# A dense phase on one Trainium2 core: fp32 products against three fp32r products of parts, and the order of its two layers

## What is computed

```python
o = o.reshape(b, n, n, D) @ W_out
h = layer_norm(x + o, ln_agg_g, ln_agg_b)
m = jax.nn.relu(h @ W1 + b1) @ W2 + b2
return layer_norm(m + h, ln2_g, ln2_b)
```

## Time and profile before

| | |
|---|---|
| median of 3 runs | 4186.32 us |
| the profiled execution | 4186.14 us |
| its span | 4184.3 us |
| TensorE busy (PE) | 3655.8 us, 87% of the span |
| VectorE busy (DVE) | 2901.9 us, 69% |
| ScalarE busy (ACT) | 2311.9 us, 55% |
| GpSimd busy (POOL) | 1372.4 us, 33% |

### The profile page before, as it was taken

How to read it: one execution, slowest core, us unless ns; L and a number is a source line. 1 busy time by engine, 2 the same in 40 slices (tenths; PEclk the granted TensorE clock), 3 DMA queues, 4 the chain that set the end, 5 groups by cost and what they waited for, 6 DMA issues and landing times. The chain is left out here.

```text
span 4184.3 us, 80451 instructions
## 1 busy us (share of the span) xinstructions
PE 3655.8 (87%) x29631; PEld 2959.3 (71%) x29631; DVE 2901.9 (69%) x4154; ACT 2311.9 (55%) x5686; POOL 1372.4 (33%) x730
## 2 busy tenths in 40 slices
PE   8873888688869997899999978999999777788887
PEld 5542666466648884788888856888888744688886
DVE  2657999699966772577777743777777644577787
ACT  3423777577754553466656643666666411477776
POOL 0355999799964441100000001000000000122254
PEclk9986999899989998999999999999999999999999
DMA  4365111411123333000000011000000133545565
GB/s 127 93 156 139 42 44 41 110 44 40 41 61 96 101 96 95 26 16 16 16 18 24 11 55 61 16 16 16 16 16 11 33 125 133 164 137 137 143 203 173
DMA packets 211175, 304.39 MB, mean 73 GB/s; under 512 B 18656, under 2 KB 156768, under 8 KB 210272
## 3 DMA queue, kind: packets, MB, share of 16 engines
q1 hardware_dynamic: 201696, 292.56, 23.5%
q10 hardware_dynamic: 9216, 8.39, 0.6%
HBM read 200.22 MB, written 100.66 MB: 72 GB/s over the span
## 5 line engine op out<-in xcount | busy, mean ns | idle before, releaser
L611 DVE TENSOR_TENSOR mp_Z<-mp_psL,mx_rv 128x2816 f32<-128x2816 f32 (+1 forms) x256 | 786.7, 3149 | 46.1 <-DMA mx_rv<-rv 25.2
L631 POOL TENSOR_TENSOR mp_Z<-mp_lvs,mx_rv 128x1280 f32<-128x1280 f32 (+1 forms) x256 | 797.0, 3730 | 64.5 <-ACT mp_lvs L554 39.8
L561 ACT ACTIVATE mp_cut<-mp_psO,mx_mask 128x128 f32<-128x128 f32 x2048 | 550.1, 403 | 157.1 <-PE mp_psO L504 157.1
L504 PE MATMUL mp_psO<-mp_Z,mp_pair 128*16 128x256 f32 x8192 | 504.7, 387 | 106.8 <-POOL mp_Z L631 93.6
L1164 PE MATMUL sv_psO<-at_v_hi,sv_p_hi 128*128 128x258 f32 x2048 | 583.3, 285 | 13.2 <-DVE sv_p_lo L1252 10.1
L1164 PE MATMUL sv_psO<-at_v_lo,sv_p_hi 128*128 128x258 f32 x2048 | 578.2, 282 | 0.0
L1164 PE MATMUL sv_psO<-at_v_hi,sv_p_lo 128*128 128x258 f32 x2048 | 577.9, 282 | 0.0
L1183 ACT COPY sv_S<-sv_psS 128x512 f32<-128x512 f32 x512 | 300.5, 587 | 395.1 <-PE sv_psS L1138 289.6
L504 PEld LDWEIGHTS mp_psO<-mp_Z,mp_pair 128*16 128x16 f32 x8192 | 339.6, 124 | 247.3 <-DVE mp_Z L611 135.3
L1227 DVE TENSOR_TENSOR sv_run<-sv_run,sv_S 128x512 f32<-128x512 f32 x448 | 314.5, 702 | 249.5 <-ACT sv_S L1183 249.0
L1252 DVE TENSOR_TENSOR sv_p_lo<-sv_S,sv_p_hi 128x512 fp32r<-128x512 f32 x512 | 353.8, 691 | 107.9 <-ACT sv_p_hi L1192 106.9
(11 more groups left out here) (199 smaller groups left out, 6888.5 us busy)
## 6 DMA issues: line engine op xcount, KB each, us to landing
re_xg<-xg SPq DMA_DIRECT2D x192, 384.0 KB, 3.3
xg<-ga_xg SPq DMA_DIRECT2D x32, 768.0 KB, 3.7
mp_pair<-att SPq DMA_DIRECT2D x128, 128.0 KB, 2.6
fr_xr<-in_x SPq DMA_DIRECT2D x16, 512.0 KB, 4.8
fr_xl<-in_x SPq DMA_DIRECT2D x32, 256.0 KB, 4.2
rv<-fr_rvs SPq DMA_DIRECT2D x16, 512.0 KB, 2.9
att<-mx_rv SPq DMA_DIRECT2D x16, 512.0 KB, 6.8
att<-fr_E SPq DMA_DIRECT2D x16, 512.0 KB, 6.4
```

Of the source, the lines that this page charges most:

```text
L504: mm = pe.matmul(psO[32 * j:32 * j + 2 * H, c % 2, q, :], pair[:, s, :, :, c * YC + y], Z[:, c, y, :], start=True, stop=True, tile_positio ...
L561: ins = nc.scalar.activation(cut[:, s, c, :, h * DK:(h + 1) * DK], psO[:, c % 2, :, h * DK:(h + 1) * DK], ACT.Copy, scale=mask[:, h:h + 1])
L611: nc.vector.tensor_tensor(Z[:, c, 0:m], psL[:, s, 0:D].unsqueeze(1).broadcast_to([P, m, D]), rv[:, c * YC:c * YC + m, :], ALU.mult).then_i ...
L631: nc.gpsimd.tensor_tensor(Z[:, c, m:YC], lvs[:, s, :].unsqueeze(1).broadcast_to([P, YC - m, D]), rv[:, c * YC + m:(c + 1) * YC, :], ALU.mu ...
```

## The change

Output projection and inner layer are made of three fp32r products each. The weights are split once, `wo_hi`, `wo_lo`, `wa_hi`, `wa_lo`. Per tile, ScalarE makes the high parts `oT_hi` and `hT_hi`, and VectorE the low parts `oT_lo` and `hT_lo`. `hT` no longer has the first norm's shift; its product with W1 is made once (8 products of one column) and added to b1, as `b1s`. The transposes of the input move to one round earlier, behind the output projection (`turn_o`), and the loads with them. The outer layer moves ahead of the inner one. `xoff` becomes two instructions of one column. An `xl`, `xT`, relu or root is as before.

```diff
@@ -655,16 +655,19 @@
...
+        wo_hi, wo_lo = (ph.sb(n, [P, KT, D], F32R) for n in ("wo_hi", "wo_lo"))
+        wa_hi, wa_lo = (ph.sb(n, [P, KT, F1], F32R) for n in ("wa_hi", "wa_lo"))
...
         g1c, b1nc = (ph.sb(n, [P, KT]) for n in ("g1c", "b1nc"))
         b1c = ph.sb("b1c", [P, MT])
+        b1s = ph.sb("b1s", [P, MT])
...
-        oT = ph.sb("oT", [P, 2, KT, W])
+        oT_hi, oT_lo = (ph.sb(n, [P, 2, KT, W], F32R) for n in ("oT_hi", "oT_lo"))
...
-        hT = ph.sb("hT", [P, 2, KT, W])
+        hT_hi, hT_lo = (ph.sb(n, [P, 2, KT, W], F32R) for n in ("hT_hi", "hT_lo"))
...
@@ -728,13 +732,19 @@
...
                 ox = o_d.rearrange("b n (y x) d -> (b n) x y d", x=2)
+
+                def load(i):
+                    reach(sp, o_turned, i - 1)
+                    reach(sp, added1, i - 1)
+                    for c in range(2):
+                        sp.dma_start(oin[c * N:(c + 1) * N, i % 2], ox[i * U:(i + 1) * U, c].rearrange("u y d -> y u d")).then_inc(in_[i % 2], 16)
+                    sp.dma_start(xres[:, i % 2], tile_rows(x.rearrange("b x y d -> (b x y) d"), i)).then_inc(in_[i % 2], 16)
+
+                load(0)
+                load(1)
                 for i in range(LAST + 1):
-                    if i < NT:
-                        reach(sp, o_turned, i - 1)
-                        reach(sp, added1, i - 1)
-                        for c in range(2):
-                            sp.dma_start(oin[c * N:(c + 1) * N, i % 2], ox[i * U:(i + 1) * U, c].rearrange("u y d -> y u d")).then_inc(in_[i % 2], 16)
-                        sp.dma_start(xres[:, i % 2], tile_rows(x.rearrange("b x y d -> (b x y) d"), i)).then_inc(in_[i % 2], 16)
+                    if i + 2 < NT:
+                        load(i + 2)
                     n = i - 4
                     if 0 <= n < NT:
                         sp.wait_ge(t_made, n + 1)
@@ -755,18 +765,30 @@
...
+                def parts(k):
+
+                    return ((0, 0, k), (0, 1, k), (1, 0, k))
+
...
+                oTs, wos, hTs, was = (oT_hi, oT_lo), (wo_hi, wo_lo), (hT_hi, hT_lo), (wa_hi, wa_lo)
                 pe.wait_ge(w_in, 16 * len(loads))
+                for f in range(MT):
+                    for k in range(KT):
+                        mm = pe.matmul(ps_m[:, f, 0:1], wa[:, k, f * P:(f + 1) * P], b1nc[:, k:k + 1], start=(k == 0), stop=(k == KT - 1))
+                mm.then_inc(b1_turned, 1)
+
+                def turn_o(i):
+                    pe.wait_ge(in_[i % 2], (i // 2 + 1) * 48)
+                    reach(pe, oT_kept, i)
+                    turn(ps_o, oin[:, i % 2], o_turned)
+
+                turn_o(0)
                 for i in range(LAST + 1):
-                    if i < NT:
-                        pe.wait_ge(in_[i % 2], (i // 2 + 1) * 48)
-                        reach(pe, oT_kept, i)
-                        turn(ps_o, oin[:, i % 2], o_turned)
                     n = i - 1
                     if 0 <= n < NT:
                         pe.wait_ge(ln[H_LN]["normed"], n + 1)
@@ -780,22 +802,34 @@
                     if i < NT:
                         pe.wait_ge(oT_kept, i + 1)
                         reach(pe, added1, i)
-                        by_token(ps_1, oT[:, i % 2], wo, KT, made1)
-                    n = i - 1
-                    if 0 <= n < NT:
-                        pe.wait_ge(hT_kept, n + 1)
-                        for f in range(MT):
-                            if f % 2 == 0:
-                                reach(pe, mT_made, (n - 1) * 2 + f // 2 + 1)
-                            for k in range(KT):
-                                mm = pe.matmul(ps_m[:, f, :], wa[:, k, f * P:(f + 1) * P], hT[:, n % 2, k, :], start=(k == 0), stop=(k == KT - 1))
-                            if f % 2 == 1:
-                                mm.then_inc(made2, 1)
+                        reach(pe, w_cut, 1)
+                        for u in range(U):
+                            terms = [t for k in range(KT) for t in parts(k)]
+                            for e, (a, c, k) in enumerate(terms):
+                                mm = pe.matmul(ps_1[:, u * D:(u + 1) * D], oTs[a][:, i % 2, k, u * P:(u + 1) * P], wos[c][:, k, :],
+                                               start=(e == 0), stop=(e == len(terms) - 1))
+                        mm.then_inc(made1, 1)
+                    if i + 1 < NT:
+                        turn_o(i + 1)
                     n = i - 2
                     if 0 <= n < NT:
                         pe.wait_ge(mT_made, n * 2 + 2)
                         reach(pe, added3, n)
                         by_token(ps_3, mT[:, n % 2], wb, MT, made3)
+                    n = i - 1
+                    if 0 <= n < NT:
+                        pe.wait_ge(hT_kept, n + 1)
+                        pe.wait_ge(w_cut, 2)
+                        pe.wait_ge(b1_made, 1)
+                        for f in range(MT):
+                            if f % 2 == 0:
+                                reach(pe, mT_made, (n - 1) * 2 + f // 2 + 1)
+                            terms = [t for k in range(KT) for t in parts(k)]
+                            for e, (a, c, k) in enumerate(terms):
+                                mm = pe.matmul(ps_m[:, f, :], was[c][:, k, f * P:(f + 1) * P], hTs[a][:, n % 2, k, :],
+                                               start=(e == 0), stop=(e == len(terms) - 1))
+                            if f % 2 == 1:
+                                mm.then_inc(made2, 1)
 
             @block.scalar
             def _(act):
@@ -808,17 +842,24 @@
 
...
+                nc.scalar.copy(wo_hi[:, :, :], wo[:, :, :]).then_inc(w_hi_cut, 1)
+                nc.scalar.copy(wa_hi[:, :, :], wa[:, :, :]).then_inc(w_hi_cut, 1)
+
+                def keep_oT_hi(i):
+                    act.wait_ge(o_turned, i + 1)
+                    reach(act, made1, i - 1)
+                    keep(oT_hi[:, i % 2], ps_o, oT_hi_kept)
+
+                keep_oT_hi(0)
                 for i in range(LAST + 1):
-                    if i < NT:
-                        act.wait_ge(o_turned, i + 1)
-                        keep(oT[:, i % 2], ps_o, oT_kept)
                     n = i - 1
                     if 0 <= n < NT:
                         act.wait_ge(h_turned, n + 1)
                         for k in range(KT):
-                            ins = nc.scalar.activation(hT[:, n % 2, k, :], ps_h[:, k * W:(k + 1) * W], ACT.Identity,
-                                                       bias=b1nc[:, k:k + 1], scale=g1c[:, k:k + 1])
-                        ins.then_inc(hT_kept, 1)
+                            ins = nc.scalar.activation(hT_hi[:, n % 2, k, :], ps_h[:, k * W:(k + 1) * W], ACT.Copy, scale=g1c[:, k:k + 1])
+                        ins.then_inc(hT_hi_kept, 1)
+                    if i + 1 < NT:
+                        keep_oT_hi(i + 1)
                     n = i - 3
                     if 0 <= n < NT:
                         root(T_LN, n)
@@ -834,10 +875,11 @@
                         root(X_LN, n)
                     n = i - 1
                     if 0 <= n < NT:
+                        act.wait_ge(b1_made, 1)
                         for f in range(MT):
                             if f % 2 == 0:
                                 act.wait_ge(made2, n * 2 + f // 2 + 1)
-                            ins = nc.scalar.activation(mT[:, n % 2, f, :], ps_m[:, f, :], ACT.Relu, bias=b1c[:, f:f + 1])
+                            ins = nc.scalar.activation(mT[:, n % 2, f, :], ps_m[:, f, :], ACT.Relu, bias=b1s[:, f:f + 1])
                             if f % 2 == 1:
                                 ins.then_inc(mT_made, 1)
                     n = i - 4
@@ -871,12 +913,35 @@
                 nc.vector.memset(eps[:, :], LN_EPS).then_inc(eps_set, 1)
                 dve.wait_ge(w_in, 16 * len(loads))
                 nc.vector.tensor_tensor(hbr[:, :], b1nr[:, :], b2r[:, :], ALU.add).then_inc(hbr_made, 1)
+                for j, (lo, full, hi) in enumerate(((wo_lo, wo, wo_hi), (wa_lo, wa, wa_hi))):
+                    dve.wait_ge(w_hi_cut, j + 1)
+                    nc.vector.tensor_tensor(lo[:, :, :], full[:, :, :], hi[:, :, :], ALU.subtract).then_inc(w_cut, 1)
+                dve.wait_ge(b1_turned, 1)
+                nc.vector.tensor_tensor(b1s[:, :], ps_m[:, :, 0], b1c[:, :], ALU.add).then_inc(b1_made, 1)
+
+                def keep_oT_lo(n):
+                    dve.wait_ge(oT_hi_kept, n + 1)
+                    nc.vector.tensor_tensor(oT_lo[:, n % 2], ps_o[:, :].rearrange("p (k t) -> p k t", k=KT), oT_hi[:, n % 2], ALU.subtract).then_inc(oT_kept, 1)
+
+                def keep_hT_lo(n):
+                    dve.wait_ge(hT_hi_kept, n + 1)
+                    for k in range(KT):
+                        ins = nc.vector.scalar_tensor_tensor(out=hT_lo[:, n % 2, k, :], in0=ps_h[:, k * W:(k + 1) * W], scalar=g1c[:, k:k + 1],
```

(19 more changed lines are left out.)

## The result

The changed kernel takes **4200.89 us** (median of 6 runs, 4198.33 to 4204.64) against 4185.11 us of the kernel before (6 runs, 4182.99 to 4189.31): a ratio of 1.0037, 95% interval 1.0024 to 1.0050. It is slower by 16 us. The forecast was 4208, in a range of 4198 to 4221. By time alone the effect is small, 0.4%, and the profile has to show where it comes from.

What follows compares the result with a forecast made beforehand. TensorE bounds the dense phase at 10.01 us a round; the move closes a loop of 10.95, so 28 rounds x 0.94 = +26.3, less 3 to 4 in the drain, together +22: 4208 us, range 4198 to 4221.

Steps and rivals of the forecast that it cites:

- The bound and the products: Dense phase: TensorE is the bound at 10.01 us a round; 12 products fall from 5.24 to 4.32 us as fp32r.
- TensorE's own work: TensorE's work in a dense round after the change: 9.08 us, or 9.24 with changes from fp32 to fp32r.
- The loop: Inner layer's end, relus 3 and 4, xl, ps_x transposes, TensorE's next round; TensorE idles about 1.6 us a round at ps_x.
- the loop's length: Time of one turn through relus, xl and TensorE: 10.87 us, 11.0 with type changes, taken as 10.95 a round.
- the two changes of type: Switches from fp32 to fp32r products on TensorE, 0.08 us lost at each of two a round.
- The transposes after a wait: Four ps_x transposes on TensorE after waiting for xl: 0.44 + 0.16 = 0.60 us.
- The second loop: From ps_x transposes through output projection, oT_hi cast, second norm's root, VectorE's norms, relus and xl: 10.75 us, 10.83 with one type change.
- The count and the drain: 28 rounds x 0.94 = +26.3 us; three last tiles drain through the norms with xoff freed, -3 to -4.
- the rival of overlaps: Overlapping steps and hand-overs shorten the loop to 10.0 to 10.3 us a round: 4182 to 4195 us; chance 7%.
- VectorE's new work: Added per round on VectorE: oT_lo 0.72 us, hT_lo pair 0.9; xoff becomes 0.3 for both instructions.
- TensorE stays the bound: Rival: ScalarE finishes relus 3, 4 and xl within the 0.44 us of ps_h transposes: 4157 us; chance 4%.
- xoff held all the same: Rival: GpSimd's multiply still holds xoff to 1.3 us, xl starts 0.9 later each round: 4233 us; chance 9%.

Runs made afterwards that it cites:

- b1: Changed kernel with ps_x transposes between outer and inner layer on TensorE, and xl one round later behind hT_hi on ScalarE; 4157.06 us, ratio 0.9935.
- e5: Changed kernel with xl made between relus 1, 2 and relus 3, 4 on ScalarE; 4184.46 us, ratio 0.9997.
- e1: Changed kernel with the ps_x transposes moved behind the next input's transposes, ahead of the outer layer; 4177.15 us, ratio 0.9983.
- e3: Kernel before, fp32 throughout, with only the outer layer moved ahead of the inner one; 4221.93 us, ratio 1.0095.
- e2: Changed kernel with the inner layer put back ahead of the outer layer on TensorE; 4189.14 us, ratio 1.0011.
- e6: e2 with the second norm's root put ahead of the cast to oT_hi on ScalarE; 4176.46 us, ratio 0.9978.
- e4: Kernel before with only xoff made as two instructions of one column; 4184.2 us, one run.
- e7: Changed kernel with xoff again made by one scalar_tensor_tensor, as in the kernel before; 4208.2 us, one run.

## Why the prediction was right, and where it was off

- **The bound and the products** held. TensorE's own work was put at 9.08 to 9.24; b1 shows 9.05. The fp32r products start 0.119 us apart (1405.48 to 1408.09, 22 steps), against my 0.12. The Trainium skill ("TensorE: Matmul & The Clock Gate", Back-to-back issue gap) gives an isolated warm gap of N/2.4 + 2.5 ns, 109 ns for 256 columns; the trace does not agree, by 10 ns a product.
- **The loop** held in every link: the two last relus, xl, ps_x, released by xl 31 times. The wait is 51.1 us in total; I had some 1.5 x 28 = 42. A steady round shows 1.47, and the rest is longer waits in the drain (5.75 us the longest). Three runs show that it was this chain: in e5 the round falls by 0.62 when two relus move, in e1 the wait for xl is gone from the steady rounds when the transposes move, and in e3 the order alone makes it.
- **The term that was mis-sized most is the loop's length**, "10.87, and 11.0 with the two changes of type ... I take 10.95". It is 10.74. The transposes after a wait cost 0.41 to the next product, not 0.44 + 0.16: 0.19 less. The added 0.16 was taken from the length of the last record, while the start of what follows is what counts. A change of type costs about nothing net: the output projection is 0.08 longer, but outer and inner layer together are 6.31 where I had 6.33 without a change. 10.87 - 0.19 + 0.08 - 0.02 = 10.74. I chose 0.21 too much, 5.5 us over 26 rounds.
- **The second loop** was shorter too, 10.26 in e2 against 10.75, mostly VectorE: 4.00 against 4.35. In the changed kernel it has slack, seen as the 0.37 that ScalarE waits for relus 3 and 4. That it is real is shown by e2, and by e6, which opens it.
- **The count and the drain.** 26 rounds are at the full length, not 28 (1.9 us). The drain gained 1.0 us up to the last xl, and lost 0.4 behind it (9.10 us to the end of the phase against 8.71), against my 3 to 4. e4 shows the size of the reason that I gave: freeing xoff alone brings the drain 1.0, not 1.0 for each of three tiles. In the changed kernel the drain differs in more than xoff: its last outer layer also took 1.7 us longer at the lower clock. So the 26.3 less 3.5 of the sum, 22.8, become 22.8 - 5.5 - 1.9 + 3.0 = 18.4.
- **What the number owes to luck.** All misses but the drain's lay on one side, and that one, 3.0, took back part of the other 7.4. The measured medians differ by 15.8, less than the phase's 18.4 or 18.9; the rest of the program varies by a few us between profiles, and that went the other way here.
- **Three slips in the sums**, none of which matters: 26.3 less 3 to 4 is 22.3 to 23.3, and was written down as 22; the terms of TensorE's own work add up to 9.09 with 3 x 0.44; and the rival of overlaps, 10.0 to 10.3 a round, gives some 4182 to 4191 by the same sum, not 4195.
- **VectorE's new work** was as priced: the pair of hT_lo to its next start 0.79 and 0.88 long (I had 0.9), oT_lo 0.60 and 0.68 (0.72), xoff 0.34 (0.3). With the products for b1 the stretch from load to first transposes is 0.6 us longer in the changed kernel, and 0.8 to 1.5 in the six other kernels that have them (I had 1); no run takes them out alone. That the first transposes begin at 1235.33 against 1235.27 says nothing of it, since the load itself was issued 0.5 us sooner. Seen from these transposes, the first output projection begins 0.7 us later, and the first xl 0.1 us later.
- **The rivals.** TensorE stays the bound: refuted. The 4157 given for it is what b1 measured (4157.06), which needed two more moves; that the two agree to 0.1 us is chance, since b1's round is 9.05 and the rival had 9.2. xoff held all the same: refuted for the changed kernel, 0.34 at the very place. The Trainium skill ("GPSIMD Engine Reference", Specifications) names two SBUF inputs as a cause of contention; the earlier trace rows and e7 agree for the fused step, 1.26 us, and one-column tensor_scalars, with no second tensor to read, are not held beside the same multiply.
- **The change taken apart:** everything but the move, in the old order, +2.8 us of phase (e2), the move alone +37.1 (e3), both +18.4. The move makes the kernel slower at either precision; what the parts save on TensorE is then spent waiting. e2 holds the parts together with the earlier transposes of the input, which put the cast ahead of the root; no run leaves these transposes where they were.

## What to carry to other kernels

When an engine is 100% busy and its work is to be cut, first add up the loops through the other engines, and only then price the cut. Here the order of the edits left circles of 9.8, 10.3 and 10.7 us beside a TensorE of 9.05, and 0.96 us of work saved a round became 0.73 us lost. In this kernel order mattered more than work. A step that the next round needs (xl) should not stand behind work that the round's last product releases, and its reader should have some us of other work ahead of it. Measure such loops from start to start, not from the ends of records. And when an edit opens one loop, the round goes to the next longest, so a round that comes out as forecast does not show which loop binds (e5, e6).

## What was not expected of the hardware

- A restart of the transposes after a wait of 1.47 us cost 0.41 us to the next product, and 0.36 without a wait (b1, 1403.24 to 1403.60): fp32r products start closer behind transposes than fp32 ones (0.44). Before fp32 products the wait costs as little, 0.49 in the drain (1570.90 to 1571.39).
- TensorE's granted clock fell to a mean of 0.67 within one layer behind an idle piece of 1.90 us in the drain, in the changed kernel and in e3, and stayed at 1.00 behind the same piece in e7; 1.47 us of idling in every round left it at 1.00. Where it fell, one layer took 1.7 us longer. So the drain of two profiles can differ by that much with the same work.
- The start of the phase varies in the same way. The granted clock from the first transposes to the first xl was 0.90 before and 0.84 in e4, whose code differs up to there only in xoff, and e4 took 0.6 us longer.
